# A routed two-expert layer behind cross attention on one core: 24 full blocks started under the last two groups' gating, pair one-hots and gates made by GpSimd, ranking one tile later

## What is computed

```python
# x: (128, 64, 128) float32, N = 8192 tokens of D = 128; ctx the same shape; mask per key
x = x + xattn(layernorm(x), ctx, ctx, mask, Wq, bq, Wk, bk, Wv, bv, Wo, bo)   # 16 heads of 8, causal
n = layernorm(x)
probs = softmax(gelu(n @ wg1 + bg1) @ wg2)            # 8 experts
top_vals, top_idx = top_k(probs, 2)                   # two experts for each token
gates = zeros.at[token, top_idx].set(top_vals)
h = gelu(einsum('nd,edh->enh', n, w_in))              # hidden size 256
o = einsum('enh,ehd->end', h, w_out)
x = x + einsum('ne,end->nd', gates, o)
```

## Time and profile before

| | |
|---|---|
| median of three runs | 621.63 us (619.68 to 622.26) |
| profiled execution | 623.75 us |
| its span, first to last instruction | 622.0 us |
| mean granted TensorE clock | 0.956 |
| busy: PE, DVE, ACT, POOL | 501.8, 481.1, 393.0, 248.8 us |
| moved by DMA | 46.87 MB, mean 75 GB/s |

### The profile page before, as it was taken

One profiled execution on the slowest core, in us unless ns is written; L12 is line 12 of the kernel. 1 busy time (PEld: TensorE's weight loads), 2 busy tenths in 40 slices (PEclk: granted clock), 3 DMA queues, 4 the chain that ended last, 5 costly groups with the idle time before them and its releaser, 6 DMA issues.

```text
span 622.0 us, 18994 instructions
## 1 busy us (share of the span) xinstructions
PE 501.8 (81%) x6640; PEld 377.4 (61%) x6640; DVE 481.1 (77%) x1629; ACT 393.0 (63%) x723; POOL 248.8 (40%) x323
## 2 busy tenths in 40 slices
PE   2579898888888888888888887411999999999992
PEld 0146555555554554554555554301999999999992
DVE  3588999999999999999999997660566666566662
ACT  2156687777777777777777676511666666566660
POOL 4131233353353354254254233340355555455552
PEclk9999999999999999999999999555999999999997
DMA  3137212212212212212110101047233334333310
GB/s 110 18 81 220 62 48 69 78 42 66 81 40 65 83 39 65 83 40 62 46 41 26 52 20 38 35 137 241 76 107 103 109 105 110 98 110 86 80 42 1
DMA packets 41805, 46.87 MB, mean 75 GB/s; under 512 B 9738, under 2 KB 33555, under 8 KB 41248
## 3 DMA queue, kind: packets, MB, share of 16 engines
q1 hardware_dynamic: 33696, 30.39, 18.7%
q0 software_dynamic: 5984, 12.90, 6.1%
q10 hardware_dynamic: 2032, 2.36, 1.3%
HBM read 28.54 MB, written 18.58 MB: 76 GB/s over the span
## 4 chain that ended last, share of the span: by engine, by line
DVE 35%; PE 34%; issue 13%; SPq 9%; DMA 2%; ACT 2%; POOL 1%; ACTq 0%; another core or an unknown queue 0%; POOLq 0%; DVEq 0%
PE probs_t L562 14%; PE bank L573 13%; DVE smax L776 9%; DVE rden L788 7%; SPq L266 5%; DVE rows L798 2%; PE scores L553 2%; DVE left L843 2%; DVE sm L780 1%; SPq L238 1%; DVE stat L753 1%; DVE stat L804 1%; DVE xT L763 1%; PE scores L377 1%; PE probs_t L393 1%
## 5 line engine op out<-in xcount | busy, mean ns | idle before, releaser
L1174 POOL DMA_INDIRECT out<-yb,token_row x91 | 89.3, 982 | 106.2 <-DVE yb L1059 65.9
L1136 POOL DMA_INDIRECT routed_rows<-rows,pos x64 | 64.3, 1004 | 122.5 <-DVE pos L879 100.9
L678 ACT ACTIVATE pt<-probs_t 128x1024 f32<-128x1024 f32 x64 | 65.5, 1023 | 60.0 <-PE probs_t L393 59.7
L717 ACT ACTIVATE hb<-probs_t 128x512 f32<-128x512 f32 x91 | 54.3, 597 | 73.2 <-PE probs_t L562 54.9
L562 PE MATMUL probs_t<-xbT,wi 128*128 128x128 f32 x728 | 98.1, 278 | 2.3 <-ACT wi L732 1.2
L377 PE MATMUL scores<-kx,qT 64*64 64x512 f32 x512 | 70.6, 621 | 36.2 <-DVE sm L780 23.9
L573 PE MATMUL bank<-wo,hb 128*128 x728 | 96.1, 275 | 0.0
L562 PEld LDWEIGHTS probs_t<-xbT,wi 128*128 128x128 f32 x728 | 90.1, 195 | 3.1 <-issue 1.7
L573 PEld LDWEIGHTS bank<-wo,hb 128*128 128x128 f32 x728 | 88.5, 192 | 0.1
L776 DVE TENSOR_REDUCE smax<-scores 128x16 f32<-128x1024 f32 x64 | 77.8, 1216 | 12.2 <-PE scores L383 10.9
L780 DVE TENSOR_TENSOR sm<-scores,smax 128x1024 f32<-128x1024 f32 x64 | 78.4, 1224 | 2.2
(11 more groups left out here) (117 smaller groups left out, 838.3 us busy)
## 6 DMA issues: line engine op xcount, KB each, us to landing
xb<-routed_rows SPq DMA_DIRECT2D x91, 132.5 KB
ctx_in<-ctx_t SPq DMA_DIRECT2D x16, 256.0 KB, 3.0
x_all<-x SPq DMA_DIRECT2D x16, 256.0 KB, 3.3
kx<-kT SPq DMA_DIRECT2D x256, 16.0 KB
routed_rows<-padding_rows SPq DMA_DIRECT2D x15, 132.5 KB
routed_rows<-padding_rows ACTq DMA_DIRECT2D x14, 132.5 KB
out<-yb,token_row POOLq DMA_INDIRECT x91
mask_in<-mask SPq DMA_DIRECT2D x16, 64.0 KB, 3.8
```

The costliest lines, as they stand in the source:

```text
L678: nc.scalar.activation(pt[:, :, :].rearrange("p j q -> p (j q)"), PT2[:, :], ACT.Copy).then_inc(s_ptev, 1)
L1136: nc.gpsimd.indirect_dma_start(out=rows_d, out_offset=bass.IndirectOffsetOnAxis(ap=pos[:, r % RR, u:u + 1], axis=0), in_=rows[:, r % RR, u ...
L1174: nc.gpsimd.indirect_dma_start(out=out, out_offset=bass.IndirectOffsetOnAxis(ap=token_row[:, b % RY:b % RY + 1], axis=0), in_=yb[:, b % RY ...
```

## The change

- GpSimd makes `sel16` as seven products of columns of `chosen` (`pair_of`), and the gates of a routed row. DVE's `coded`, `code`, `sel16` and gate instructions go. DVE waits for GpSimd's products of the group before, ahead of `probs` and `chosen`.
- `rank_tokens(s - 3)` runs in tile 0 of body s (it was tile 3 of body s - 1), `count_tokens` and `positions` in tile 1 (was 0), and the scatters move along.
- The tables are made twice. The first time, in body 15, from the counts of the groups 0 to 12 with counts divided by 128 and rounded down, which gives at least 24 full blocks; after `write_tables(0)` these 24 blocks start. `start_second_part` moves each bin's first row past what the first part took; the second tables, for 67 blocks, take the rest, rounded up.
- The gating of groups 14 and 15, their counting, the second tables and the scatters are put between the blocks 0 to 14 by hand (`last_gates`, `PAIR_AT`, `SCATTER_AT`).
- All 28 padding transfers are issued by SP, in two halves, before the loads of the block groups 4 and 5 (blocks 16 to 19, 20 to 23). Each is written as 16 long rows in place of 128.
- x is held in a ring of 6 groups (`x_in`); a load of x waits for the residual of the group that was in its slot. The rings of `xb` and `yb` become 10 and 10 (8 and 6 before).

```diff
+EARLY = 13
+NA = 24
+PART_OF = (0, NA)
+NBS = (NA, NB - NA)
-ROUND = float(1 << 23)
+ROUND = float(3 << 22)
+RR_X = 6
+PADS_BEFORE = (4, 5)
-RX = 8
+RX = 10
-RY = 6
+RY = 10
+PAIR_AT = (1, 8)
+SCATTER_AT = (4, 11)
...
                 def load_x(s):
+                    if s >= RR_X:
+                        sp.wait_ge(s_res, U * (s - RR_X + 1))
...
+                            sp.dma_start(rows_d[bass.ds(at, BLK), :].rearrange("(a r) w -> a (r w)", a=16),
+                                         pad_c.ap().rearrange("(a r) w -> a (r w)", a=16)).then_inc(s_pad, 16)
...
+                    if first == PART_OF[p]:
+                        if p:
+                            sp.wait_ge(s_pad, 16 * (NP + 1))
                         for i in range(RR):
-                            sp.wait_ge(s_scat[i], 16 * U * (NS // RR))
+                            sp.wait_ge(s_scat[i], 16 * U * len(range(i, NS if p else EARLY, RR)))
...
-                sp.wait_ge(s_tails, 1)
-                pad_regions(mybir.EngineType.SP, sp, PAD_SP)
-                sp.wait_ge(s_tabd, 1)
                 for g in range(len(GROUPS)):
+                    if g in PADS_BEFORE:
+                        if g == PADS_BEFORE[0]:
+                            sp.wait_ge(s_tails, 1)
+                        half = PADS_BEFORE.index(g)
+                        pad_regions(range(half * NP // 2, (half + 1) * NP // 2))
                     load_group(g)
...
# PE, attention loop
+                        if u == 3 and s == NS - 1:
+                            turn_table(0)
...
                             if u == 0 and runs(s, 3):
+                                rank_tokens(s - 3)
+                            if u == 1 and runs(s, 3):
                                 pe.wait_ge(s_pch, CNT * (s - 3) + 2)
                             if u == 1 and runs(s, 2):
                                 gate_logits(s - 2)
-                            if u == 3 and runs(s, 2):
-                                rank_tokens(s - 2)
                             project_o(t - 1)
...
# PE, behind down(b)
+                def last_gates(b):
+                    if b == 0:
+                        pe.wait_ge(s_res, NT)
+                        pe.wait_ge(s_pch, CNT * (NS - 3) + 2)
+                        gate_logits(NS - 2)
+                    if b == 3:
+                        pe.wait_ge(s_rge, NS - 1)
+                        transpose_rows(NS - 1)
+                        pe.wait_ge(s_lsh, NS - 1)
+                        rank_tokens(NS - 2)
+                    if b == 5:
+                        gate_hidden(NS - 1)
+                    if b == 7:
+                        pe.wait_ge(s_pch, CNT * (NS - 2) + 2)
+                        gate_logits(NS - 1)
+                    if b == 10:
+                        pe.wait_ge(s_lsh, NS)
+                        rank_tokens(NS - 1)
+                    if b == 13:
+                        turn_table(1)
...
# ACT, between gelus(b) and the copy for block b + 2
+                def last_gates(b):
+                    if b == 0:
+                        gate_exp(NS - 2)
+                        ln2_norm(NS - 1)
+                    if b == 3:
+                        xt2_evac(NS - 1)
+                    if b == 5:
+                        gate_gelu(NS - 1)
+                    if b == 7:
+                        gate_exp(NS - 1)
-                act.wait_ge(s_tails, 1)
-                pad_regions(mybir.EngineType.Activation, act, PAD_ACT)
...
# DVE
+                    if r:
+                        dve.wait_ge(s_gate, r)
                     link(4, nc.vector.tensor_tensor(probs[:, :, :], ex[:, :, :], wide(r_inv), ALU.mult))
...
+                    if r:
+                        dve.wait_ge(s_sel, r)
                     nc.vector.tensor_tensor(chosen[:, :, :], left[:, :, :], probs[:, :, :], ALU.not_equal
                                             ).then_inc(s_chosen, 1)
...
-                        if u == 0 and runs(s, 3):
+                        if u == 1 and runs(s, 3):
                             dve.wait_ge(s_y, t - 1)
                             count_tokens(s - 3)
+                            positions(s - 3)
+                            if s == EARLY + 2:
+                                dve.wait_ge(s_cum, 1)
+                                blocks_of_bins(0)
...
+                        if u == 2 and s == EARLY + 2:
+                            ends_of_bins(0)
+                            bins_of_blocks(0)
...
# DVE, behind gated(b)
+                def last_gates(b):
+                    if b == 0:
+                        choose(NS - 2)
+                    if b == 3:
+                        count_tokens(NS - 2)
+                        positions(NS - 2)
+                    if b == 7:
+                        choose(NS - 1)
+                    if b == 10:
+                        count_tokens(NS - 1)
+                        dve.wait_ge(s_pch, CNT * (NS - 1) + 2)
+                        nc.vector.tensor_copy(tails[:, :], run_s[:, :]).then_inc(s_tails, 1)
+                        positions(NS - 1)
+                    if b == 11:
+                        blocks_of_bins(1)
+                        ends_of_bins(1)
+                    if b == 12:
+                        bins_of_blocks(1)
+                    if b == 14:
+                        write_tables(1)
...
# GpSimd
+                def pair_of(r):
+                    pool.wait_ge(s_chosen, r + 1)
+                    if r:
+                        pool.wait_ge(s_rank, r)
+                        pool.wait_ge(s_pch, CNT * (r - 1) + 3)
+                    at = 0
+                    for a in range(E - 1):
+                        n = E - 1 - a
+                        last = nc.gpsimd.tensor_tensor(sel16[:, :, at:at + n], chosen[:, :, a + 1:E],
+                                                       chosen[:, :, a:a + 1].broadcast_to([P, U, n]), ALU.mult)
+                        at += n
+                    last.then_inc(s_sel, 1)
+                    nc.gpsimd.tensor_tensor(rows[:, r % RR, :, GATE:GATE + E], chosen[:, :, :], probs[:, :, :], ALU.mult
+                                            ).then_inc(s_gate, 1)
...
                 for b in range(NB):
+                    if b in PAIR_AT:
+                        pair_of(NS - 2 + PAIR_AT.index(b))
+                    if b in SCATTER_AT:
+                        r = NS - 2 + SCATTER_AT.index(b)
+                        rows_complete(r)
+                        scatter_rows(r, range(U))
                     scatter_out(b)
```

More of the change, by code:

```diff
@@ L132, in build @@
         run_s, routing = sb("run_s", [P, NP]), sb("routing_s", [P, NR])
-        region_s, experts_s, bits, codes, base, row_no, token_rows = (
-            routing[:, place[k]] for k in ("region", "experts", "bits", "codes", "base", "row", "token"))
-        x_all = sb("x_all", [P, NT, D])
+        experts_s, base, row_no, token_rows, first_row = (
+            routing[:, place[k]] for k in ("experts", "base", "row", "token", "first"))
+        x_in = sb("x_in", [P, RR_X, U, D])
         ctx_in = sb("ctx_in", [P, RING, U * P])
@@ L167, in build @@
         r_max, r_sum, r_inv = (sb(n, [P, U]) for n in ("r_max", "r_sum", "r_inv"))
-        chosen, coded, code = sb("chosen", [P, U, E]), sb("coded", [P, U, E]), sb("code", [P, U])
+        chosen = sb("chosen", [P, U, E])
         sel16 = sb("sel16", [P, U, NP], F16)
@@ L226, in build @@
         s_tok, s_part = (sem(n) for n in ("token_rows_ready", "first_expert_added"))
-        PAD_SP, PAD_ACT = range(0, NP // 2), range(NP // 2, NP)
-        def pad_regions(engine, queue, bins):
-            for first in range(bins.start, bins.stop, NP // 4):
-                _, values = nc.values_load_multi_w_load_instructions(
-                    tails[0:1, first:first + NP // 4], engines=[engine], min_val=0, max_val=ROWS - BLK,
-                    skip_runtime_bounds_check_because="made on the chip by counting into existing regions")
-                for k in range(NP // 4):
-                    start = (first + k) * REG
-                    at = nc.s_assert_within(values[k], start, start + N,
-                                            skip_runtime_bounds_check_because="a region holds all tokens")
-                    queue.dma_start(rows_d[bass.ds(at, BLK), :], pad_c.ap()).then_inc(s_pad, 16)
         (s_bt, s_bte, s_up, s_gl, s_dn, s_gm, s_gt, s_yb) = (sem(n) for n in (
@@ L313, in _, with pad_regions @@
                     body(s, s // 2, s % 2)
+                def pad_regions(bins):
+                    for first in range(bins.start, bins.stop, NP // 4):
+                        _, values = nc.values_load_multi_w_load_instructions(
+                            tails[0:1, first:first + NP // 4], engines=[mybir.EngineType.SP], min_val=0, max_val=ROWS - BLK,
+                            skip_runtime_bounds_check_because="made on the chip by counting into existing regions")
+                        for k in range(NP // 4):
```

(26 more changed lines are left out.)

193 lines of the change are left out of this document (84 added, 109 removed).

## The result

The changed kernel takes 618.02 us in the median (616.37 to 622.24, 20 executions). The kernel before takes 621.67 beside it (618.76 to 625.01, 20 executions). The ratio is 0.995, with a 95% interval of 0.9932 to 0.9968. So the change makes the kernel faster, by 0.5%, where 1.6% was forecast. The profiled execution took 617.17 us with a span of 615.4; 612.0 had been forecast for the span. On one chip (experiment 7) some executions fell into a slower state, and the times and ratios given there leave them out.

The account below looks back on a forecast made before the run. DVE was taken to bound the attention loop, PE the expert stage, with a serial gap between. 622.0 - 9.9 - 29.7 + 20.6 + 9.0 = 612.0 us span, 611.6 median; forecast 603 to 618 (0.55), range 600 to 623.

Parts of the forecast that it names:

- three signs of a wrong forecast: Attention bodies staying at 23 us, down products 3.9 apart beyond block 3, or SP's halves of pads over 14 us.
- What bounds the kernel: DVE's instructions set the attention loop, PE the expert stage, with a serial gap between where PE does almost nothing.
- Part 1: Attention loop: instructions leaving DVE for GpSimd save 0.76 us in each of 13 bodies, 9.9 us; GpSimd's products stay hidden.
- Part 2: Start of the blocks: tables made in body 15 let the first up product start near 403.7, 29.7 us earlier.
- Part 3: Between the first blocks: inserted gating, table steps and clock make PE wait, +20.6 us, bounds 13 and 28.
- Part 4: Pads on SP delay the loads of blocks 16 and 20: +3.1, +3.5 and 2.4 for the clock, +9.0 us.
- the pad: In part 4, a pad of 16 long rows on SP taken at 0.55 us; the old one took 0.68.
- rivals A: Pads fit: 0.4 us or less each on SP, part 4 worth 0 to 1, clock back by block 2; 601; chance 0.17.
- the clock: In part 4, PE's clock falling behind the waits for late blocks, 2.4 us.
- Rival C: SP's pads cost 13.19 us a half or more; blocks 16 and 20 late, part 4 costs 24; median 626.6; chance 0.09.
- rival B: PE's clock stays low in the early blocks: fourteen blocks near 3.9 us each cost 28; median 619; chance 0.14.
- From span to median: Final step from the forecast span of 612.0: median 0.4 under the span, 611.6; profiled run 1.75 above, 613.8.

Follow-up runs that it names:

- experiment 7: Changed kernel with ACT's weight copies and group 15's norm ahead of gating steps (first kernel): 636.14 us; also combined: 622.4; kernel before: 625.7.
- experiment 2: Changed kernel with DVE making pair one-hots and gates again, all else as changed: 628.71 us, ratio 1.0123.
- experiment 1: Kernel before with only GpSimd's pair one-hots and gates and ranking one tile later; tables, pads, blocks as before: 616.17 us, ratio 0.9942.
- experiment 10: Kernel before, unchanged, run again on another chip: 620.1 us, span 618.2.
- experiment 5: Changed kernel with SP issuing 14 pads before group 5 and 7 before group 6, ACT the last 7: 605.01 us, ratio 0.9758.
- experiment 9: combined and its twin with 24 already met waits added to DVE, on a further chip: 600.19 and 601.94 us, ratios 0.9698 and 0.9704.
- combined: Kernel of experiment 5 with ACT's weight copies and group 15's norm ahead of gating steps, ACT's pads one block later: 622.4, 604.08, 600.19 us on three chips.

## Why the prediction was right or wrong

The gain is 3.7 us where 10.0 was forecast, and 618.02 lies at the upper end of the forecast, 603 to 618. None of the three signs of a wrong forecast came: bodies take 22.2 us, the down products don't stay 3.9 apart beyond block 3, and SP's halves stay under 14 us. What failed is a size.

**What bounds the kernel**: right. DVE's instructions set the body: 0.76 us less of them gave 0.76 us (22.97 to 22.21), and experiment 2 gave them back.

**Part 1** (9.9 us): right. The products took 1.50 us (1.26 + 0.24), just below the lower bound of 1.6, and the one-hots were there in time. Experiment 2 measures 10.6. What the prediction didn't see is that in the old serial gap GpSimd's place in the order would have bitten (experiment 1); the change escapes it by having blocks run there.

**Part 2** (up(0) 39.6 us earlier, with part 1): right, 40.6. About 2.4 us of it come from the stall of the earlier trace rows, which the trace after doesn't have; against 431.12 of experiment 10 it is 38.2. So the close match is partly luck. One of its steps doesn't add up either: 395.8 + 3.6 - 1.95 - 0.76 - 1.21 is 395.5 for the end of the last normalisation, not the 394.4 that was used, and 394.3 is what came (384.36 with part 1's 9.9 added).

**Part 3** (20.6 us): right in size and place. From the distances of the down products: block 0 +5.0 (put at 6.2), the clock behind it +1.5 (1.5), block 3 +2.0 (2.0), block 5 +1.7 (1.5), block 7 +4.2 with the clock (3.1), blocks 10 to 14 +4.7 (6.3), where for the last of these I take experiment 5's distances (2.4 and 3.2), since the pads cover them in the changed kernel. Sum 19.1. The errors are of both signs and partly cancel, and the terms given for blocks 10 to 14 add up to 6.0, not 6.3. GpSimd's scatters cost nothing, as said. Gating steps inserted between blocks could be priced from the rows of before, instruction by instruction.

**Part 4** (9.0 us): **this is the step that failed.** Of the 35.5 us between the down products it holds what part 3 leaves, 16.4 (35.5 - 19.1). Experiment 5 shows 11.6 of them to be SP's pads. Three of its terms were too small:
- the pad, 0.55, taken because a pad of sixteen long rows might issue faster. It issues in 0.50 like the old one and costs 0.68. The earlier trace rows said just that, and the prediction noted that the issue might not depend on the rows, but gave that only to rivals A and C. 14 x 0.13 = 1.8 us a half.
- the register loads, two at about 1.2: 2.9 us a half, 0.5 more.
- so the halves took 12.6 and 13.2 instead of 10.3 (the prediction's own terms make 10.1). A half that is 2.6 late on average passes its delay to block 16 and again to block 20. Block 16 landed 15.9 us behind the tails (449.0 - 433.13, the chain's step at L1089) where 13.8 was put, and PE wanted it after 8.7 instead of 10.7, since the table steps held it up less. These 4 us are the difference between the 3.1 forecast and the 7.14 measured. Block 20 waited 5.31 instead of 3.5.
- the clock: behind the first wait two down products came 1.9 and 1.0 us late, behind the second one 1.7, in all 4.6 against 2.4.

The waits are 4.0 and 1.8 too long and the clock 2.2; some 0.6 us of this lies on terms of part 3 that the waits cover. That makes the 7.4 us by which part 4 was too small.

Rival C had exactly this mechanism, at 13.19 us a half, but it put 24 us on it. Its waits of 9 and 10 us came out at 7.14 and 5.31. The point at which it would have eaten the gain, 14.5 us a half, wasn't reached, and the change stays faster. The Trainium skill (TensorE: Matmul & The Clock Gate, HAM oscillation) stood behind rival B; this trace agrees in kind, with half clock behind PE's waits of 3.58, 7.14 and 5.31 us. It does not show the size of B: the clock was back within three blocks each time, and nowhere stayed low for fourteen.

**From span to median.** The trace after is 615.4, the forecast 612.0: up(0) 1.0 better than forecast, the blocks behind it 4.4 worse (34.0, which is the 35.5 less the 1.5 of the late block 52 that the trace of before has and the trace after hasn't, against 29.6). The median is worse by 6.4. The other 3.0 us come from the step that carried the span over to the median: the profiled execution of before stood 2.1 above its median, so I took the median 0.4 below the span. In the changed kernel the median (618.02) lies 2.6 above the profiled span, and in experiment 10 1.9 above (620.1 and 618.2). The profiled execution of before, at 623.75, was slower than 18 of the 20 executions in the result, and its trace has 3.5 us of stalls that the one of experiment 10 lacks; that most executions lack them is likely, not shown. The row that shows one of them was there, `<-remote` in the earlier trace rows, and I used the time without asking what it was. So of the 6.4 us, 3.4 are the span's, with part 4 as its cause, and 3.0 this step's.

Against the undisturbed trace of before (618.2) the measured terms close: 618.2 - 9.9 - 28.3 + 19.1 + 16.4 = 615.5, and the trace after has 615.4. This is a balance of what was measured, not a forecast. The 28.3 is the 38.2 of part 2 less part 1's 9.9.

## What to carry to other kernels

Overlapping a serial gap with the next stage pays only what its transfers leave: count every issue that moves onto a queue at the full distance from one to the next in the trace (0.68 us here, not 0.50), add the reads of addresses, and compare the sum with what the ring of loads behind them covers; if it doesn't fit, split the issues between two queues, one for each block of work (12.6 us here). Have an engine do for the next stage first what doesn't depend on the wait (ACT's copies ahead of its gating, 2.3 to 5.1 us). And before a sum is made against a profiled execution, look for idle time without a releaser in it, and take a second trace where there is some.

## What the hardware showed that I had not expected

- The issue of a transfer from DRAM to DRAM with its address in a register takes 0.50 us on SP whether it has 128 rows or sixteen long ones.
- Behind a wait of 2.2 us PE's clock fell to half in one execution and not in another of the same program (experiment 9). The program took 604.74 and 598.33 us in two of its executions on one chip.
- DVE and ACT stood together for 0.8 us in nearly each attention body on one chip, in `combined` and in experiment 7's first kernel; `combined` did not have it on two others. In the kernel before, DVE stands for some 2 us with the same label near the end of the loop, in two of three traces. No record names the releaser, and a shift of DVE's instructions took nothing away where there was no stall. The shift, and the changed kernel, were not run on the chip that had the stalls, so the cause stays open.
